# DLRM tower on one core: in 16 of 32 units of a chunk the embeddings are stationary, the weights stream, and the sums run along rows

## What is computed

```python
e = jnp.stack([tbl_0[ids[:, 0]], ..., tbl_31[ids[:, 31]]], axis=1)      # (512, 32, 64)
pw = jnp.einsum('bpi,pij->bpj', e[:, ids_x, :], w)
z = jnp.einsum('bpj,bpj->bp', pw, e[:, ids_y, :])                        # (512, 496)
h = jnp.concatenate([z, dense_ctx], axis=1)                              # (512, 512)
h = jnp.maximum(h @ W_top1 + b_top1, 0.0)                                # 512
h = jnp.maximum(h @ W_top2 + b_top2, 0.0)                                # 256
y = h @ W_top3
```

## Time and profile before

| what | value |
|---|---|
| median of 3 runs | 408.5 us (407.29 to 408.74) |
| the profiled execution's own time | 407.67 us |
| its span, from the first to the last instruction | 405.9 us |
| TensorE busy (matmul, weight load) | 238.7 us, 212.4 us |
| VectorE busy | 156.0 us |
| ScalarE busy | 20.6 us |
| GpSimd busy | 121.1 us |
| mean granted TensorE clock | 1.000 |

### The profile page before, as it was taken

How to read it: one execution, slowest core, us unless ns; L and a number is a source line. 1 busy time by engine, 2 the same in 40 slices (tenths; PEclk the granted TensorE clock), 3 DMA queues, 4 the chain that set the end, 5 groups by cost and what they waited for, 6 DMA issues and landing times.

```text
span 405.9 us, 9496 instructions
## 1 busy us (share of the span) xinstructions
PE 238.7 (59%) x4368; PEld 212.4 (52%) x4368; DVE 156.0 (38%) x187; ACT 20.6 (5%) x58; POOL 121.1 (30%) x132
## 2 busy tenths in 40 slices
PE   0502000100003111139999999999999999999996
PEld 0401000100003000018888788989999999999985
DVE  0101000100001000105767674677774777855871
ACT  1000000000000000000000101000001001011001
POOL 5777777777777777000000000000000000000000
DMA  6778811111111111000000000000000000000000
GB/s 188 231 236 245 319 27 28 26 26 26 26 26 28 27 27 26 3 0 2 3 2 4 2 3 2 3 2 3 2 3 4 2 3 3 3 2 2 4 3 3
DMA packets 7594, 15.97 MB, mean 39 GB/s; under 512 B 2817, under 2 KB 3073, under 8 KB 7298
## 3 DMA queue, kind: packets, MB, share of 16 engines
q1 hardware_dynamic: 3458, 11.15, 8.2%
q0 software_dynamic: 4096, 4.20, 5.2%
HBM read 15.34 MB, written 0.00 MB: 38 GB/s over the span
## 4 chain that ended last, share of the span: by engine, by line
PE 58%; issue 37%; DMA 2%; POOL 1%; ACT 1%; DVE 0%; DVEq 0%
PE pu L341 32%; PE pz L358 17%; PE pt L325 3%; PE pt L365 3%; PE pt L374 2%; POOL emb L197 1%; DMA emb<-in_tbl,idx 1%; ACT eT L207 1%; PE pt L381 1%; PE pu L413 0%; DMA idx<-in_ids 0%; DVE prod L262 0%; PE pu L374 0%; PE pt L413 0%; PE pu L419 0%
## 5 line engine op out<-in xcount | busy, mean ns | idle before, releaser
L262 DVE TENSOR_TENSOR prod<-pu,eT 128x1024 f32<-128x1024 f32 (+3 forms) x160 | 147.6, 977 | 239.3 <-remote 157.8
L341 PE MATMUL pu<-eT,ws 64*128 64x128 f32 x2048 | 133.5, 285 | 107.4 <-issue 104.0
L341 PEld LDWEIGHTS pu<-eT,ws 64*128 64x128 f32 x2048 | 124.2, 196 | 117.4 <-issue 112.8
L197 POOL DMA_INDIRECT emb<-in_tbl,idx x128 | 120.9, 945 | 41.1 <-issue 38.7
L358 PE MATMUL pz<-prod,select 128*32 128x128 f32 x2048 | 71.7, 278 | 41.5 <-issue 41.5
L358 PEld LDWEIGHTS pz<-prod,select 128*32 128x32 f32 x2048 | 57.7, 111 | 51.4 <-issue 48.4
L207 ACT COPY eT<-pt 128x128 f32<-128x128 f32 (+2 forms) x32 | 12.0, 374 | 300.9 <-remote 148.5
L325 PE MATMUL pt<-identity,emb 128*128 128x128 f32 x64 | 15.0, 316 | 14.4 <-DMA emb<-in_tbl,idx 12.9
L325 PEld LDWEIGHTS pt<-identity,emb 128*128 128x128 f32 x64 | 7.5, 145 | 18.5 <-issue 14.3
L365 PE MATMUL pt<-zT,w1s 128*128 128x128 f32 x96 | 11.5, 278 | 0.0
L365 PEld LDWEIGHTS pt<-zT,w1s 128*128 128x128 f32 x96 | 10.9, 192 | 0.4
(11 more groups left out here) (19 smaller groups left out, 9.3 us busy)
## 6 DMA issues: line engine op xcount, KB each, us to landing
ws<-in_w SPq DMA_DIRECT2D x16, 512.0 KB, 4.1
emb<-in_tbl,idx POOLq DMA_INDIRECT x128
denseT<-in_dense SPq DMA_DIRECT2D x1, 1024.0 KB
w1s<-in_w SPq DMA_DIRECT2D x1, 1024.0 KB
w2s<-in_w SPq DMA_DIRECT2D x1, 512.0 KB
idx<-in_ids SPq DMA_DIRECT2D x1, 64.0 KB, 1.9
identity<-in_ident SPq DMA_DIRECT2D x1, 64.0 KB, 2.1
w3s<-in_w SPq DMA_DIRECT2D x1, 1.0 KB
```

What stands on the lines that cost most here:

```text
L197: nc.gpsimd.indirect_dma_start(out=emb[:, c, x, :], out_offset=None, in_=tables[x], in_offset=bass.IndirectOffsetOnAxis(ap=idx[:, c, x:x + ...
L262: nc.vector.tensor_tensor(p[:, banks, slots, :], u[:, banks, slots, :], e, ALU.mult).then_inc(mult_done, 1)
L341: i = nc.tensor.matmul(pu[:, t % UR, bank, slot, :], ws[rows, u, slot, :], eT[rows, k, cols(c)], start=True, stop=True)
```

## The change

In each chunk 16 of the 32 units, all of kind "four", are *turned*. For them

- `products` issues 2 matmuls instead of 8: 128 columns of `eT` are stationary and 512 columns of `ws` stream. The result has the batch row on the partition, and along the row 16 groups (8 per bank) of 64 elements.
- `multiply` multiplies by `emb` itself instead of `eT` and writes `turned`, a ring of 6 (`RB`).
- there is no sum on TensorE. `row_sums` adds each group of 64 along the row: on ScalarE by 16 activations with `accum_out`, on VectorE by one `tensor_reduce` of 1024 elements. `BY_VECTOR` gives VectorE 8, 5, 5 and 6 of the 16 units in the four chunks, and ScalarE the other 8, 11, 11 and 10. The sums land in `zB`, batch row on the partition.
- per chunk two transposes (`transpose_z`) and one copy by ScalarE (`copy_z`) bring `zB` into half of `zT`. The other half comes from `pz`, which has half its size; the dense features lie in that half.

All users of `pt` (transposes of embeddings, of z, and the layers) now stand in one list (`USERS`), with one semaphore `pt_read`. Transposes are issued ahead of their first use by 1, 3, 4 and 4 steps in the four chunks; the MLP stands at units 8 (z), 12, 16 and 19 of the next chunk. `PR` falls from 8 to 6. The sums of four units follow two steps after the last of the four.

```diff
+TURNED = [2, 3, 4, 6, 8, 10, 12, 15, 16, 18, 20, 22, 24, 25, 26, 28]
+BY_VECTOR = [(0, 1, 2, 3, 6, 9, 12, 15), (2, 5, 8, 11, 15), (2, 5, 8, 11, 15), (2, 5, 8, 11, 13, 15)]
-PR = 8
+PR = 6
+RB = 6
+AHEAD = [1, 3, 4, 4]
+MLP_AT = {"z": 8, "l1": 12, "l2": 16, "l3": 19}
+SUMS = {min(NS, step_a(SB * i + SB - 1) + 2): i for i in range(BCH * NA // SB)}
...
+            def row_sums(b):     # scalar
+                act.wait_ge(mult_done, mults(step_b(b)))
...
+                for v in range(16):
+                    t = turned[:, b % RB, v, :]
+                    i = nc.scalar.activation(t, t, ACT.Copy, accum_out=zB[:, b // NT % 2, b % NT * 16 + v:b % NT * 16 + v + 1])
+                i.then_inc(rows_act, 1)
...
             for t in range(-1, NS):
-                for g in TURNS[t]:
-                    copy_x(g)
...
+                for user in TURNS[t]:
+                    through_pt(*user)
+                for b in range(BCH * NT):
+                    if step_b(b) == t - 1 and not by_dve(b):
+                        row_sums(b)
+            copy_z(last)
...
+                if i in TURNED:     # vector, in multiply(t)
+                    b = c * NT + TURNED.index(i)
...
+                    e = emb[:, c:c + 1, 2 * m:2 * m + 8, :].rearrange("p o f i -> p o (f i)").broadcast_to([P, 2, 4 * P])
+                    nc.vector.tensor_tensor(turned[:, b % RB, :, :].rearrange("p (x f) i -> p x (f i)", x=2),
+                                            u.rearrange("p x s i -> p x (s i)"), e, ALU.mult).then_inc(mult_done, 1)
+                    return
...
+            def row_sums(b):     # vector
...
+                nc.vector.tensor_reduce(zB[:, b // NT % 2, b % NT * 16:b % NT * 16 + 16], turned[:, b % RB, :, :],
+                                        axis=AXIS.X, op=ALU.add).then_inc(rows_dve, 1)
...
+                if u in TURNED:     # tensor, in products(t)
+                    for bank in range(2):
+                        rows = slice(EMB * bank, EMB * (bank + 1))
+                        i = nc.tensor.matmul(pu[:, t % UR, bank, :, :], eT[rows, UNITS[u][1], cols(c)], ws[rows, u, :, :],
+                                             start=True, stop=True)
+                    i.then_inc(u_ready, 1)
+                    return
```

More of the change, by code:

```diff
@@ L35, with step_a, step_b, by_dve @@
 NU = len(UNITS)
+NS = BCH * NU
+TURNED = [2, 3, 4, 6, 8, 10, 12, 15, 16, 18, 20, 22, 24, 25, 26, 28]
+SUMMED = [u for u in range(NU) if u not in TURNED]
+NT, NA = len(TURNED), len(SUMMED)
 ZCH = 4
-ZU = NU // ZCH
-NS = BCH * NU
-assert NU == 32 and ZCH * P == FIELDS * (FIELDS - 1) // 2 + DENSE
+ZA = 2
+ZU = NA // ZA
+Z_ORDER = [z for z in range(ZCH) if z != ZA - 1] + [ZA - 1]
+assert NU == 32 and NT == 16 and all(UNITS[u][0] == "four" for u in TURNED)
+assert ZCH * P == FIELDS * (FIELDS - 1) // 2 + DENSE
+BY_VECTOR = [(0, 1, 2, 3, 6, 9, 12, 15), (2, 5, 8, 11, 15), (2, 5, 8, 11, 15), (2, 5, 8, 11, 13, 15)]
+def step_a(a):
+    return a // NA * NU + SUMMED[a % NA]
+def step_b(b):
+    return b // NT * NU + TURNED[b % NT]
+def by_dve(b):
+    return b % NT in BY_VECTOR[b // NT]
+def rows_done(b, dve):
+    return sum(by_dve(v) == dve for v in range(b + 1))
 def slot_of(u, bank, slot):
@@ L288, in _ @@
                 multiply(t)
[L289 to L293, removed]
+                for b in range(BCH * NT):
+                    if step_b(b) == t - 1 and by_dve(b):
+                        row_sums(b)
+                if t > NU and t % NU == 3:
+                    z_rows(t // NU - 1, 0, ZA)
+                if t == Z_EARLY:
+                    z_rows(last, 0, ZA - 1)
+            z_rows(last, ZA - 1, ZA)
             dve.wait_ge(h1_ready, BCH)
@@ L408, in _ @@
+            transpose_z(last)
             pe.wait_ge(z_out, BCH)
-            pt_free(NG, last, last, last)
+            pt_free("l1", last)
             pe.wait_ge(mult_done, mults(NS - 2))
-            for n in range(N1):
-                for z in range(ZCH - 1):
-                    nc.tensor.matmul(l1_out(last, n), w1s[:, z, n * P:(n + 1) * P], zT[:, z, cols(last)],
-                                     start=(z == 0), stop=False)
-            for v in range(NS - SB, NS):
-                sums(v)
@@ L417, in _ @@
[L417 to L423 removed]
+            layer1(last, Z_ORDER[:-1])
+            sums_of(BCH * NA // SB - 1)
+            pe.wait_ge(z_out, BCH + 1)
+            layer1(last, Z_ORDER[-1:])
```

221 lines of the change are left out of this document (125 added, 96 removed).

## The result

| | before | after |
|---|---|---|
| median (range, executions) | 408.5 us (407.29 to 408.74, 5) | 420.58 us (419.01 to 426.44, 5) |
| ratio after/before, 95% interval | | 1.029 [1.027, 1.032] |

The forecast was 385 us with a range of 367 to 402, and 0.84 on faster. It is outside, on the other side. The profiled execution of the kernel after is the 426.44 us one, with a span of 424.5; the others lie at 419.0 to 420.6, so its places in time are read here and its last per cent is not.

A forecast was written before the change was run, and what follows sets the result against it. After the first stage TensorE bounds the kernel before; afterwards ScalarE would in chunks 1 and 2, TensorE in chunk 3. Span 184.3 + 39.5 + 49.1 + 49.1 + 47.5 + 13.6 = 383.1, so 385 us, range 367 to 402.

The forecast's parts named there:

- Queues: ScalarE's in-order work: `eT` copies wait behind row sums of 3.84 us, costing TensorE 6 us in chunk 0.
- Chunks: Length of later chunks: 47.6 + 1.5 = 49.1 us for chunks 1 and 2, 46.0 + 1.5 = 47.5 for chunk 3.
- ScalarE's pitch: Time between ScalarE's 64-element activations with accumulator: 0.24 us taken, 3.84 us a unit; 0.21 to 0.26 had chance 0.40.
- The upper bound: ScalarE activation: 0.42 us if the accumulator's output is its own instruction and neither overlaps.
- ScalarE is heavy: Rival: activations 0.29 us or more apart make the change lose, 437 us at 0.34; chance 0.12 shared with unoverlapped TensorE banks.
- banks that don't overlap: Rival on TensorE: a turned unit costs twice 0.9 us, 14 us more a chunk, 426 us; chance 0.12 shared with heavy ScalarE.
- the 46.0 of the forecast: TensorE's work a chunk: 53.9 - 8.2 + 0.3 = 46.0 us, with 0.90 us a turned unit.
- coupling: TensorE and VectorE waiting for each other, as VectorE becomes almost as full: 1.5 us a chunk.
- the ring of three: Buffers between TensorE and VectorE: TensorE (1.14 us a unit) fills them in products, as VectorE needs 1.35 with reduces.
- First stage: Until 184 us: 2.8 us a record, so units 0 to 9 through instead of 0 to 5; rival by columns, 391 us, 0.12.
- Chunk 0 and the tail: Rest of chunk 0 after the slow start 39.5 us, ending at 223.8; final layers and sums 13.6 us.
- The listed chances: Outcome probabilities: 0.40, 0.22, 0.12, 0.08, 0.12, 0.06, 0.03; faster by over 0.5% 0.84, within 0.03, slower 0.13.

The follow-up runs named there:

- a_none: Kernel after with one 64-element activation or reduce per turned unit on ScalarE and VectorE, other row sums left out: 229.83 us where the kernel before takes 255.
- a_actnone: Kernel after with one activation instead of 16 per unit on ScalarE, VectorE's reduces whole: 239.33 us where the kernel before takes 255.
- a_copyv: Kernel after with the copies to `eT` of chunks 1 to 3 moved from ScalarE to VectorE: 405.56 us, ratio 0.996 to the kernel before.
- a_ahead: Kernel after with transposes issued 5, 12 and 12 steps ahead in chunks 1 to 3 instead of 3, 4, 4: 411.98 us, ratio 1.015 to the kernel before.
- a_half: Kernel after with 8 instead of 16 activations in each ScalarE row sum, other sums left out: 389.21 us, ratio 0.953 to the kernel before.
- t8: Kernel after with 8 instead of 16 turned units a chunk and other ring sizes, transpose lead unchanged: 400.96 us, ratio 0.984 to the kernel before.
- t8_act: Kernel after with 8 turned units a chunk, earlier transposes, all row sums of chunks 1 to 3 on ScalarE: 399.15 us, ratio 0.981 to the kernel before.

## Why the prediction was wrong

**What failed is the step "Queues", and "Chunks" that took it over.** It says that 3 or 4 steps ahead "covers one row sum but not units 24, 25 and 26 in a row", prices late copies in chunk 0 at 6 us, and then gives chunks 1 to 3 no price for them at all: 49.1 is ScalarE's sum of work plus 1.5. Measured, an interval of 60.5 splits like this: 47.6 without row sums (`a_none`), + 2.6 for the reduces (`a_actnone`), + 10 for ScalarE's row sums, of which moving the copies away gives back 8 to 9 (`a_copyv`). The copy came 8.6 us after its transposes (283.82 to 292.45), and only two units, 2.06 us, stood between them and the next use of `pt`; TensorE idled 6.5 us. "Queues" counted the lead up to the first use of `eT`; what ran out first here was the lead up to the next use of `pt`. Nor could ScalarE use the time: it ran dry while TensorE caught up (3.5 of 10 us), so its 47.6 us of work, as forecast, didn't fit into 47.6 us. The sum of the fullest engine is a lower bound, and the two engines took turns being late.

**The clock was in no term.** After each stall TensorE came back at a granted clock of 0.50 to 0.66, and three units took 2.2 and 2.5 us more than at the full one behind the two large stalls, and the unit at 245.03 about 1 us more (2.08 us for a turned unit). In chunk 1 this is 3 to 4 of 65.4 us. In the kernel before TensorE had no gap in the second stage, and its mean granted clock was 1.000, so its rows couldn't show this price.

**ScalarE's pitch: right.** 0.24 was taken, and 0.239 measured; 16 activations take 3.83 us against 3.84. The upper bound's premise (an instruction of its own for the accumulator) came true, its conclusion (that neither overlaps) didn't. The rival "ScalarE is heavy" forecast the right side for the wrong reason: its condition, a pitch from 0.29 on, didn't hold. The estimate from the page "ScalarE: Activation LUTs", section "What ACT_TABLE_LOAD costs", of the Trainium skill, 0.146 us, is too low for an activation with an accumulator: the run shows 0.239.

**TensorE: nearly right.** The rival of banks that don't overlap, 1.8 us a turned unit, is out. Two turned units in a row take 1.99 us in the chain (at 194.87), so 1.0 each where 0.90 was taken; 16 times 0.1 is as much as the difference between the 47.6 of `a_none` and the 46.0 of the forecast.

**VectorE: work right, coupling short.** The reduce takes 1.207 us, alone in its group, for the 1.13 taken. VectorE is busy 43.3 us in an interval, as worked out (43.2). The coupling was put at 1.5 us a chunk; `a_actnone` shows 2.6 above `a_none`. That VectorE's reduces act through the ring of three, as the prediction has it, no run shows by itself.

**First stage: that the rate goes by records was right, the time of unit 2 wasn't.** In the timeline of the kernel after, unit 2, now turned, is issued at 67.69 and multiplied at 77.78: 10.1 us for four records, where a unit of 16 took 45:

```profile
67.69 2.08 PE L427 MATMUL pu<-ws,eT 64*128 64x512 f32 x4 [41.79 <-issue]
...
77.78 1.23 DVE L331 TENSOR_TENSOR turned<-pu,emb 128x1024 f32<-128x1024 f32 x1 [12.71 <-issue]
...
105.78 1.23 DVE L331 TENSOR_TENSOR turned<-pu,emb 128x1024 f32<-128x1024 f32 x1 [11.65 <-remote]
...
150.58 1.35 DVE L345 TENSOR_TENSOR prod<-pu,eT 128x512 f32<-128x512 f32 x3 [42.45 <-remote]
```

Four records of 512 columns are no slower than four of 128. Only units 0 to 7 were through at 184 instead of 0 to 9, because unit 1, not turned and issued at 23.41, was multiplied only at 63.77, and the count began there and not at 32.4. So unit 2 came at 77.78 and not near the 44 that was to show it. In `a_ahead` and `a_half` unit 1 was multiplied at 30.11 and 27.43, in `t8` at 66.22, so this delay is there in some executions and not in others; its cause stays open.

**Chunk 0 and the tail: near.** Chunk 0 ended at 230.3 instead of 223.8, of which the two units of the first stage are 2.5. The tail took 14.5 for 13.6. The 5.9 us by which chunk 3 is above its 47.5 no run takes apart.

**The range** took in ScalarE's pitch at both bounds and the first stage, the two costs that the rows didn't show. The cost that decided was in the order of instructions, which the diff shows in full: `row_sums` before the next `through_pt` on one engine that takes its work in the order written. The listed chances add up to 1.03 and not to 1; the three at the end (0.84, 0.03, 0.13) do add up. A slower kernel had 0.13, and for a pitch or banks that didn't come true: the order of work had no chance of its own.

## What to carry to other kernels

When long work is moved to an idle engine, list the short work already on it that another engine waits for, and price each as the longest run of long work ahead of it minus the lead; the sum of busy times says nothing of it. Move the short work to another engine or split the long work before judging the idea: here moving the copies alone turned +2.9% into -0.4%, and half the amount of moved work, with other edits, into -1.9% (`t8_act`). Where a full engine gets a gap, ask what its clock does after the gap as well.

## What the runs showed of the hardware that was not expected

- On some chips GpSimd's gathers go with a TensorE that finishes a record every 2.8 us (0.7 after the last gather), 408 us in all; on two others the same program takes 255 us. The granted clock doesn't show it (9 in each of the first 15 slices of the kernel after, with the rate at its slowest). With 32 gathers instead of 128, and plain transfers for the rest, the time fell from 408 to 279 us in one execution.
- The slow rate is one per record, whatever its columns: 10.1 us for four of 512 columns.
- After TensorE had idled for 6.51 us its granted clock was 0.66 in the 10 us that hold the restart, and 0.50, the lower level, in the 10 us around the other large stall.
- An ACTIVATE of 64 elements with an accumulator (243 ns) and the reading of that accumulator (189 ns) have a common pitch of 0.239 us.
- A tensor_reduce of 1024 elements takes 1.207 us, that is, the time of a product of 1024.
